# Three pieces of the path sums and recurrences ahead of the second alignment's first codes in a perceiver block

## The reference, cut to what matters

```
x = x + align(context, layernorm(x))      # dynamic time warping, per batch
x = x + rwkv(layernorm(x))                # sigmoid-gated recurrence over 64 steps
x = x + moe(layernorm(x)) + shared(...)   # top 2 of 8 experts, and a shared one
```

## Time and profile before

| what | us |
|---|---|
| median of 3 executions | 1174.21 |
| lowest and highest of them | 1173.29, 1180.53 |
| the profiled execution, its own time | 1176.61 |
| its span in the trace | 1175.4 |
| mean granted TensorE clock, share of full | 0.938 |

### The profile page before, as it was taken

One profiled execution on the slowest core, in us unless ns is written; L12 is line 12 of the kernel. 1 busy time (PEld: TensorE's weight loads), 2 busy tenths in 40 slices (PEclk: granted clock), 3 DMA queues, 4 the chain that ended last, 5 costly groups with the idle time before them and its releaser, 6 DMA issues.

```text
span 1175.4 us, 15523 instructions
## 1 busy us (share of the span) xinstructions
PE 1005.5 (86%) x4892; PEld 598.2 (51%) x4892; DVE 660.5 (56%) x2311; ACT 494.2 (42%) x847; POOL 115.5 (10%) x150
## 2 busy tenths in 40 slices
PE   5886639888891799997899699887999999999998
PEld 2332213333330455553576465645676767676776
DVE  4994949999999776487669612427311111111116
ACT  4885627766781345423242155243222222222221
POOL 1000000000000000000000000000252425242210
PEclk9998979999996799988899799799999999999999
DMA  9999954565876989440050097394121212123115
GB/s 354 324 309 272 274 155 141 154 190 157 237 225 163 327 252 329 135 150 11 1 186 1 0 336 249 104 349 174 49 83 57 83 56 84 56 84 105 32 52 182
DMA packets 123806, 190.47 MB, mean 162 GB/s; under 512 B 9008, under 2 KB 93136, under 8 KB 123728
## 3 DMA queue, kind: packets, MB, share of 16 engines
q1 hardware_dynamic: 117840, 171.13, 47.0%
q0 software_dynamic: 5888, 18.36, 5.1%
HBM read 165.43 MB, written 24.03 MB: 161 GB/s over the span
## 4 chain that ended last, share of the span: by engine, by line
PE 55%; DVE 29%; DMA 6%; issue 4%; ACT 3%; SPq 2%; POOL 0%; DVEq 0%; ACTq 0%; POOLq 0%
PE bank L1816 13%; PE bank L1663 8%; PE bank L1847 7%; PE bank L1684 4%; DVE table L825 4%; PE bank L1808 3%; DMA spaced<-dist 3%; DVE beyond L841 3%; DVE passed L846 3%; PE bank L1827 3%; DVE col_min L818 2%; DVE z L756 2%; PE bank L1590 2%; PE bank L1839 2%; PE bank L1811 2%
## 5 line engine op out<-in xcount | busy, mean ns | idle before, releaser
L1028 DVE TENSOR_TENSOR hid<-bank,act_s 128x352 f32<-128x352 f32 x104 | 54.2, 524 | 220.9 <-PE bank L1816 182.1
L1816 PE MATMUL bank<-w_up,srcT 128*128 x512 | 162.9, 460 | 0.8 <-ACT srcT L1434 0.8
L1574 PE MATMUL bank<-sq,ones 128*64 128x402 f32 (+1 forms) x512 | 101.3, 517 | 38.2 <-ACT sq L1291 38.2
L1442 ACT ACTIVATE act_s<-bank 128x352 f32<-128x352 f32 x104 | 47.9, 463 | 198.4 <-PE bank L1816 127.7
L1816 PEld LDWEIGHTS bank<-w_up,srcT 128*128 128x128 f32 x512 | 96.0, 189 | 47.9 <-issue 4.1
L1590 PE MATMUL bank<-table,ident 128*128 128x402 f32 x144 | 68.5, 560 | 56.3 <-DVE stays L789 51.0
L1568 PE MATMUL bank<-ctxT,latT 128*64 128x402 f32 (+1 forms) x512 | 101.2, 517 | 4.8 <-DMA ctxT<-ctx_tr_dram 4.0
L1663 PE MATMUL bank<-rows_c,on_path 128*64 128x256 f32 (+1 forms) x832 | 100.8, 395 | 2.4 <-DMA rows_c<-ctx_nat_dram 1.6
L1291 ACT ACTIVATE sq<-ctxT 128x1608 f32<-128x1608 f32 x64 | 97.5, 1526 | 8.5 <-DMA ctxT<-ctx_tr_dram 8.5
L1847 PE MATMUL bank<-w_dn,hidT 128*128 (+1 forms) x384 | 93.6, 380 | 0.4 <-DVE y_sb L1042 0.4
L1328 ACT ACTIVATE code<-bank,unpassed 128x402 bf16<-128x402 f32 x72 | 42.1, 589 | 122.9 <-PE bank L1592 122.9
(11 more groups left out here) (292 smaller groups left out, 1619.5 us busy)
## 6 DMA issues: line engine op xcount, KB each, us to landing
rows_c<-ctx_nat_dram SPq DMA_DIRECT2D x32, 896.0 KB
ctxT<-ctx_tr_dram SPq DMA_DIRECT2D x32, 804.0 KB, 8.7
ctxT<-ctx_tr_dram SPq DMA_DIRECT2D x32, 797.0 KB, 7.5
rows_c<-ctx_nat_dram SPq DMA_DIRECT2D x32, 640.0 KB
spaced<-dist SPq DMA_DIRECT2D x128, 101.0 KB, 3.8
w_up<-w_t_dram SPq DMA_DIRECT2D x16, 704.0 KB, 13.3
table<-spaced SPq DMA_DIRECT2D x48, 202.0 KB, 4.2
w_dn<-w_t_dram SPq DMA_DIRECT2D x16, 256.0 KB, 5.8
```

What stands on the lines that cost most here:

```text
L1028: e.tensor_tensor(hid[i][:, :], psum[2 * i + 1][:, 0:HH], act_s[i][:, :], ALU.mult).then_inc(hid_done, 1)
L1574: last = e.matmul(ps[b * T:(b + 1) * T, 0:nq], ones[:, 0:T], sq[i][:, b, k, 0:nq], start=False, stop=(k == KC - 1))
L1816: last = e.matmul(psum[2 * i + m][:, 0:HH], srcT[t % 2][:, k, :], w_up[:, bass.ds(ex, 1), m, k, columns], start=(k == 0), stop=(k == KC - 1))
```

## The change

`behind_second` gave no piece before n = 6. Now two pieces go behind step 0 and one behind step 4, on all three engines; every later n gives what it gave, so all later pieces stand three pieces earlier against the alignment's steps. On VectorE the one-step pause that stood behind the first four pairs' adds now stands ahead of them: these four adds come only two pieces earlier, everything behind them three.

```
 def behind_second(n):
 
     if n < 6:
-        return 0
+
+        return {0: 2, 4: 1}.get(n, 0)
     if n < 33:
         return min((n - 6) % 4, 1)
...
-            interleave(align(1), chain(add_rows(range(0, 4)), pause(), together(recurrence(0), add_rows(range(4, 8))),
+            interleave(align(1), chain(pause(), add_rows(range(0, 4)), together(recurrence(0), add_rows(range(4, 8))),
                                        beside(recurrence(1), chain(pause(), experts(RUNS[0] + RUNS[1])), shared_beside)),
                        behind_second)
```

## The result

The changed kernel takes **1179.57 us** as the median of 20 executions (1175.68 to 1183.20), beside 1174.47 us for the kernel before in the same measurement (20 executions, 1170.08 to 1180.53). The ratio is 1.0040, with a 95% interval of 1.0028 to 1.0051: some 5 us slower. That is inside the 1% that the prediction called no change, but outside its range, 1169 to 1179, and well resolved by this many executions. The forecast was 1174.4 us.

A forecast was written before the change was run, and what follows sets the result against it. VectorE's backtracking sets the pace from 609 to 666, TensorE waits for loads at the start; -4.1 in the middle, +3.8 and +0.5 in the tail sum to +0.2 us, 1174.4 us as median, range 1169 to 1179.

The forecast's parts named there:

- Part 1: Start of the moved sums: halves wait for loads until 389.9 and 397.9; second pair at 407.9, TensorE 0.5 us behind.
- Tail: Behind the second chunk's gate: four backtracking steps of 0.94 us left over, +3.8, and +0.5 waiting for half tiles.
- First chunk: Its sum of squares reaches VectorE 1.05 us earlier, with one code group fewer ahead; few waits from there to 530.
- The part of the step on the store: Before the second chunk's norm: the 0.81 us issue wait behind the first chunk's store goes; start 2.1 us earlier, at 528.7.
- last 0.3 us: Start of the second chunk: a further 0.3 us taken off in reaching 528.7, without a stated reason.
- Second chunk: Between its two kv: 8.4 us instead of 12.5; next kv at 561.3, -3.9; gate at 604.8 instead of 608.92.
- a loss of 2.1 us: Second chunk, norm to first kv: low clock and code groups take back the 2.1 us; kv stays at 552.8.
- The sum against one execution: Total of +0.2 us set on the profiled 1176.61 us, which lay 2.4 above the median: 1176.8 there, 1174.4 as median.
- Rival 1: First pair: loads come early enough, VectorE's wait of 7.29 us goes and nothing takes it back: 1166.9 us; chance 0.1.
- Rival 2: Gate doesn't come earlier, code groups between the kv being hidden; tail costs +3.8 and 0.5: 1178.5 us; chance 0.22.
- Rival 3: TensorE stays at 1.2 GHz through the second half and first two code groups: +5.5, 1179.9 us; chance 0.08.

The follow-up runs named there:

- the tail given back: Changed kernel, its three pieces of lead given back between the 84th and 92nd step, so the second chunk's gate follows 21 backtracking steps: 1173.15 us, 0.9998.
- head: Kernel before, with only the first pair's three pieces moved ahead of the codes, everything from the second pair on as before: 1180.37 us, 1.0033.
- tail: Kernel before, with one piece more behind each of steps 78, 81 and 84, so the gate stands behind 17 backtracking steps: 1178.41 us, 1.0035.
- the late shift: Kernel before up to step 63, three pieces earlier by step 66, given back before the end: 1171.34 us, 0.9976; timed again 1171.40 us, 0.9982.

## Why the prediction was wrong, point by point

**Part 1, when the sums can start: mechanism right, a little undersized.** Load 1 made TensorE wait until 390.66, load 3 until 399.21, the second pair started at 408.54. Measured from the path terms, to take out where the whole trace lies, that is 29.03 us, and before 410.46 - 378.73 = 31.73; less the 3.1 us of two more code groups it is 0.4 us behind at equal work, forecast 0.5. Over four traces each the second pair starts 31.7, 29.1, 32.2 and 32.0 us after the path terms in before (mean 31.3) and 29.0, 29.2, 31.0 and 31.1 in the change (mean 30.1), late in the two in which the second half ran at a lower clock. That is 1.9 us behind at equal work.

**Tail: right.** "Four steps of 0.94 are left over: +3.8", and +0.5 behind it: 4.3 us. Measured +4.4 in the first trace, +4.8 on the average of four, 4.1 and 4.9 by the two runs that test it alone.

**First chunk: the step that failed.** The prediction said: "its sum of squares comes to VectorE at 499.02, with one group fewer ahead: -1.55 + 0.5 = -1.05", and from there that the second chunk starts 2.1 us earlier. Up to the chunk's first kv that holds, -0.8 us. But on the average of four traces each, counted from the path terms, the sum of squares comes at 119.6 us instead of 118.5, 1.1 later. Pieces that move forward don't take code groups away, they only let them fall elsewhere, and the sum followed them only at the places where they left. One row per stretch shows it, with the matmuls of L1592 (one for each code group) as the count. In each row stand the stretch, its length, the busy time of PE and PEld on that line alone, then TensorE's granted clock, DMA share, GB/s. First the kernel before, then the changed one (its L1593), from the path terms to chunk 1's gate, cut as in the table above and at the fourth add:

```profile
378.73:441.57 62.84, 4.54 (x13) 1.36 (x13) 0.87 0.94 294
441.57:477.95 36.38, 2.33 (x7) 0.67 (x7) 1.00 0.96 301
477.95:522.47 44.52, 2.00 (x6) 0.58 (x6) 0.91 0.33 104
522.47:552.74 30.27, 2.75 (x7) 0.84 (x7) 0.80 0.27 83
552.74:565.22 12.48, 0.92 (x3) 0.29 (x3) 1.00 0.00 0
565.22:608.92 43.70, 0.00 (x0) 0.00 (x0) 0.88 0.29 96
```

```profile
379.51:439.64 60.13, 3.67 (x11) 1.06 (x11) 0.88 0.98 306
439.64:474.97 35.33, 2.33 (x7) 0.67 (x7) 1.00 0.98 312
474.97:521.19 46.22, 2.50 (x7) 0.73 (x7) 0.96 0.37 115
521.19:550.94 29.75, 2.54 (x7) 0.73 (x7) 0.89 0.20 61
550.94:560.29 9.35, 0.33 (x1) 0.10 (x1) 1.00 0.00 0
560.29:603.70 43.41, 0.92 (x3) 0.29 (x3) 0.96 0.30 101
```

Both columns of counts sum to 36. Two groups leave the first stretch and two leave the stretch between chunk 1's kv; one turns up in the third stretch and three in the last. In the last they cost nothing (43.41 against 43.70). In the third they do. TensorE's timeline there, first of the kernel before:

```profile
493.05 0.90 PE L1590 MATMUL bank<-table,ident 128*128 128x402 f32 x2
...
496.23 2.75 PE L1730 MATMUL bank<-ones,val 128*128 128x1 f32 x16 [1.44 <-ACT val L1406]
498.85 6.20 PE L1742 MATMUL bank<-w_o,kv 128*128 128x256 f32 x16
...
515.76 0.84 PE L1590 MATMUL bank<-table,ident 128*128 128x402 f32 x2
...
518.03 1.09 PE L1754 MATMUL bank<-ident,hn 128*128 128x128 f32 x8 [0.59 <-DVE hn L717]
```

Then of the changed one:

```profile
474.77 0.84 PE L1591 MATMUL bank<-table,ident 128*128 128x402 f32 x2
...
494.87 2.04 PE L1731 MATMUL bank<-ones,val 128*128 128x1 f32 x16 [3.12 <-ACT val L1407]
496.77 1.69 PE L1591 MATMUL bank<-table,ident 128*128 128x402 f32 x2
498.25 1.55 PE L1592 MATMUL bank<-col_min,less 128*128 128x402 f32 x2
...
499.93 3.67 PE L1743 MATMUL bank<-w_o,kv 128*128 128x256 f32 x16
...
515.83 0.91 PE L1591 MATMUL bank<-table,ident 128*128 128x402 f32 x2 [1.71 <-DVE stays L790]
...
517.42 1.04 PE L1755 MATMUL bank<-ident,hn 128*128 128x128 f32 x8
```

The group at 474.77 stands between the two kv (13.63 us apart, before 12.11). The one at 496.77 stands between the squares and the output product, at the low clock. Before, that group stood ahead of the squares (493.05), where TensorE had to wait for ScalarE in any case: that wait is 1.44 us behind the group, and 3.12 us now that the group no longer stands there. Behind the squares it takes 3.2 us, of which some 1.5 us reach VectorE, since the product behind it is then faster (3.67 us instead of 6.20). The one at 515.83, in front of the gate product, needs forward steps that VectorE has not done yet, and TensorE waits 1.71 us for them. Little of that wait is a cost: the crossing behind it (517.42) needs VectorE's last piece of the second norm, which ends only at 516.90, so the group delays it by 0.5 us.

Over four traces each, the stretch from first kv to gate grows by these parts: +1.5 us between the two kv, +0.4 from there to the squares, +1.5 from the squares to VectorE's last add of the output product (5.5 us before, 7.0 now), +0.4 to the last piece of the second norm, and -0.5 from that piece to the gate; together +3.3. The other runs bear it out. In the three other kernels that shift the first chunk (everything earlier but nothing ahead of the codes, the pause where it was, the tail given back) the stretch takes 48.0, 47.8 and 46.2 us, as it takes 46.2 to 48.8 in the changed one. In all ten traces without that shift, whatever else was changed, it takes 42.2 to 44.5.

So on the average the first chunk's gate comes 2.5 us *later*, and the second chunk's norm starts 1.7 us later (151.6 us after the path terms, before 149.9) instead of 2.1 earlier. The part of the step on the store was right: the pause in front of that norm, 0.45 to 0.91 us in the four traces of before, is gone in all four of the changed kernel, and gate to norm takes 7.5 us instead of 8.3. (The last 0.3 us that the prediction takes off beside it has no row behind it.) The two first traces alone would not have shown the failure, for in them the first chunk's gate comes 2.1 us earlier (141.7 against 143.7): the trace of before is the slowest of its four up to there.

**Second chunk: mechanism right.** "Next kv at 561.3 instead of 565.22, -3.9": the interval shrank by 3.1 us in every trace, forecast 12.5 to 8.4, found 9.3. TensorE's group is followed by 0.69 us of waiting for ScalarE. But the forecast had it start from an unchanged first kv (552.8), having allowed for a loss of 2.1 us in front of it; the traces have it start 2.3 us later. Of the 2.1 lost between the norm's start and kv only 0.6 showed (21.7 us before, 22.3 now), which made up for part of the first chunk's error. The gate product is 1.3 us earlier, not 4.1. That is 2.8 us of the miss.

**The sum against one execution.** The prediction took 2.4 us off, since its profile lay above the median. The four traces of before average 1172.9 us of span, so the subtraction was fair as far as it goes. But the first trace has its excess between path terms and first gate, 143.7 us where the four average 141.6, which is the stretch that the change rearranges. There each term, -1.05 among them, was set against an execution that is 2 us over the mean there. With terms as the traces average them the sum is -1.3 + 4.8 = 3.5 us, and 4.7 us was measured. The remaining 1.2 us is within what the means of four traces leave open (their spans differ by 5.9 us within before), and isn't explained.

**The rivals.** Rival 1, the idle is really used: false; the pair's loads are what it waits for. Rival 2, slower by what is left over, 1178.5 us, decided by a gate later than 604.6 us: nearest to what happened, in its mechanism and its time. Its sign can't decide, though: the gate stands at 603.7, 606.3, 604.8 and 606.1 us in the four traces of the change, and in those of before at 608.9, 603.1, 605.3 and 606.4. Its stated reason, that the distance between the two kv doesn't shrink, was wrong; what kept the gate late was the first chunk. Rival 3, a cold start kept: in two of the four traces the second half's 24 matmuls take 4.36 and 4.50 us instead of 2.81, the granted clock being below its high level, and the codes behind them run at the high one. It is worth 1.6 us when it happens. The Trainium skill, "TensorE: Matmul & The Clock Gate", section "HAM oscillation — how this bites in real kernels", describes a loop in which every wait for a transfer between short bursts of matmuls puts the array back to half rate; by that both halves here would be slow each time. The trace agrees for the first half (4.93, 4.77, 5.82 and 6.21 us for 28 matmuls, 3.24 at the high clock) and for the second in half of the traces.

**Parts added up.** The runs that do one part alone give: head +3.9 us (1.0033), tail +4.1, the late shift -2.8 and -2.1. Their sum is about 5.5, the change as a whole 4.7 to 4.8, with some 2 us of uncertainty in each term. No run shifts the first chunk alone, so the sum has no term for the step that failed, and that it comes near the whole is partly luck. Two other combinations don't settle that term's share of the time: everything earlier without the head (+2.7 us), less tail and late shift, leaves about +1; the change with the tail given back (-0.2), less head and late shift, leaves about -1.7. What the step costs is read from the traces, not from these medians. The head's +3.9 stands beside +1.9 up to the fourth add in its two traces, so its size is less sure than its sign.

## What to carry to other kernels

Where two streams share an engine by a table, moving one forward takes no piece of the other away, it only puts the pieces elsewhere. Write down how many stand in each stretch before and after, for all stretches, and price them where they arrive as well as where they leave. A piece that filled a wait costs nothing; the same piece behind the release has to be paid for. Work put in front of a release is only as good as its own inputs; a half of the sums that waits for its load holds up the codes that stand behind it in TensorE's order (VectorE waited 11.29 us in place of 7.29). And what a shift leaves over at the far end, where one engine alone sets the pace, is paid in full (four steps of 0.94 us here): give the tail its old distances back before judging the rest. For effects of some 5 us in 1175, take three or four profiles of each kernel, since two single ones can differ with the wrong sign.

## What the runs showed of the hardware

The same program gets its clock back at different times from one execution to the next. The kernel before ran its first 28 sum matmuls in 4.93 us in three profiles and in 3.24 in one, behind the same codes and an idle stretch of 27 us; the first add came 2.6 us earlier in that one (23.08 us after the path terms, 25.69 in the first trace). The same holds behind a wait of 2 to 3 us for a load: 24 matmuls took 2.81 us in two profiles of the changed kernel, 4.36 and 4.50 in the two others. In the eight traces that have both halves ahead of the codes it goes with the first half: where its 28 matmuls took 4.77 to 4.97 us (four traces), the 24 behind the wait took 2.81; where they took 5.66 to 6.21 us (the four others), the 24 took 4.36 to 4.50, at a granted clock of 0.62 to 0.64, although it was 0.96 to 1.00 during the wait. What makes the first half take the longer or the shorter time isn't seen in the traces.
